# A four-layer decoder kernel: four batches in work in the first self-attention, and layer 1's cross weights prepared ahead

## The reference

```python
qkv = einsum('bsh,oh->bso', layernorm(x), w_qkv) + b_qkv
q, k, v = split(qkv, 3)
probs = softmax(q @ k.T / sqrt(256))
out = (probs @ v) @ w_out.T + b_out
```

## Time and profile before

| | us |
|---|---|
| median of 3 runs (lowest to highest) | 4235.8 (4234.36 to 4239.09) |
| profiled execution, its own time | 4226.08 |
| its span, first to last instruction | 4224.3 |
| mean granted clock of PE | 0.894 of full |
| `L0_attn` | 22.3 to about 200 |
| `L1_attn` | about 1124 to 1323 |
| `L1_xattn` before its first batch | 1323.6 to 1377.0 |

### The profile page before, as it was taken

One profiled execution on the slowest core, in us unless ns is written; L12 is line 12 of the kernel. 1 busy time (PEld: TensorE's weight loads), 2 busy tenths in 40 slices (PEclk: granted clock), 3 DMA queues, 4 the chain that ended last, 5 costly groups with the idle time before them and its releaser, 6 DMA issues. The chain is left out here.

```text
span 4224.3 us, 79122 instructions
## 1 busy us (share of the span) xinstructions
PE 3331.4 (79%) x29439; PEld 2439.1 (58%) x29440; DVE 2628.3 (62%) x6901; ACT 1752.5 (41%) x3882; POOL 102.1 (2%) x111
## 2 busy tenths in 40 slices
PE   5677777734485888988988989387997889768999
PEld 4545555411264556656656666166886767544788
DVE  4454454488667677777677766776884178577033
ACT  2234434357422566666666666133333244221011
POOL 0000000000001000000000000000110000000000
PEclk9899999855697999999999999698888999889599
DMA  2000000000300000000000000200000000023100
GB/s 88 13 16 20 21 16 21 7 0 0 127 11 10 2 1 2 1 1 2 1 2 1 1 2 1 86 0 11 15 15 1 0 1 0 27 73 90 42 9 11
DMA packets 85463, 79.13 MB, mean 19 GB/s; under 512 B 12496, under 2 KB 78640, under 8 KB 84784
## 3 DMA queue, kind: packets, MB, share of 16 engines
q1 hardware_dynamic: 84096, 75.57, 6.0%
q10 hardware_dynamic: 1200, 1.11, 0.1%
HBM read 74.57 MB, written 2.10 MB: 18 GB/s over the span
## 5 line engine op out<-in xcount | busy, mean ns | idle before, releaser
L2927 PE MATMUL bank<-L1w_w,L1x_xqT 128*128 128x512 f32 x640 | 303.2, 597 | 1.4 <-DVE L1x_xqT L3221 1.4
L2990 PE MATMUL bank<-L1w_wp,L1x_catT 128*128 128x256 f32 x1024 | 244.0, 381 | 12.0 <-ACT L1x_catT L3104 12.0
L1031 ACT ACTIVATE L0x_P<-bank,L0x_level 128x512 f32<-128x512 f32 x256 | 155.1, 688 | 189.9 <-PE bank L981 189.9
L3227 DVE TENSOR_REDUCE L1x_ssq<-L1x_square 128x4 f32<-128x512 f32 x192 | 131.6, 685 | 147.1 <-ACT L1x_square L3066 143.2
L3098 ACT ACTIVATE L1x_cat<-bank,L1x_osum 128x128 f32<-128x128 f32 x512 | 146.3, 369 | 170.1 <-DVE L1x_osum L3258 170.1
L2990 PEld LDWEIGHTS bank<-L1w_wp,L1x_catT 128*128 128x128 f32 x1024 | 186.8, 190 | 49.2 <-ACT L1x_catT L3104 15.0
L1047 DVE TENSOR_REDUCE L0x_top<-bank 128x4 f32<-128x512 f32 x256 | 158.9, 683 | 75.4 <-PE bank L959 73.7
L2975 PE MATMUL bank<-L1x_v,L1x_PT 128*128 128x129 f32 x1024 | 147.2, 286 | 65.4 <-ACT L1x_PT L3093 65.4
L3066 ACT ACTIVATE L1x_square<-bank 128x512 f32<-128x512 f32 x192 | 115.6, 602 | 160.9 <-PE bank L2927 160.9
L3076 ACT ACTIVATE L1x_hatT<-bank,L1x_affine 128x512 f32<-128x512 f32 x192 | 148.7, 774 | 71.1 <-PE bank L2949 69.0
L2949 PEld LDWEIGHTS bank<-ident,L1x_hat 128*128 128x128 f32 x768 | 91.0, 143 | 149.3 <-DVE L1x_hat L3237 114.0
(11 more groups left out here) (647 smaller groups left out, 8066.5 us busy)
## 6 DMA issues: line engine op xcount, KB each, us to landing
L0x_mask<-in_maskrows SPq DMA_DIRECT2D x16, 512.0 KB, 3.7
L3w_wg<-in_L_ffn_Wg SPq DMA_DIRECT2D x8, 704.0 KB, 8.5
L3w_wu<-in_L_ffn_Wu SPq DMA_DIRECT2D x8, 704.0 KB, 10.2
L1w_wp<-in_L_xattn_wproj SPq DMA_DIRECT2D x1, 4096.0 KB, 29.6
L3x_ctxT<-in_ctxT SPq DMA_DIRECT2D x32, 128.0 KB, 2.1
L3w_wd<-in_L_ffn_Wd SPq DMA_DIRECT2D x8, 512.0 KB, 10.0
...
```

The lines of the kernel that those rows point to most:

```text
L1031: act.activation(self.P[:, i % 2, r, :], self.work_bank[r][:, :], ACT.Exp, bias=self.level[:, :]).then_inc(self.p_ready.sem, 1)
L2927: last = pe.matmul(made_bank[n % 4][:, :], inputs(SOURCE[n], k), w[:, k, 4 * n:4 * n + 4, :], start=(k == 0), stop=(k == C - 1))
L2990: last = pe.matmul(y_bank[:, 0:D], catT[:, j, :], wp[:, 4 * m + j, :], start=(m == 0 and j == 0), stop=(m == MG - 1 and j == 3))
L3227: dve.tensor_reduce(ssq[:, 4 * n:4 * n + 4], square[:, n % 2, :].rearrange("p (h e) -> p h e", h=4), X, ALU.add).then_inc(sum_ready.sem, 1)
```

## The change

It does four things.

1. **`L0_attn`** is written in turns with a lead of three batches (`staged_by(eng, turn, 3)`: three turns in front, a loop of two turns run six times, four behind). In turn b PE turns xn(b+3), mixes b, scores b+1, projects b+2 in two halves with the transpose of o(b) between them, projects the output of b and transposes P(b+1). `norm_vector` moves from DVE to POOL. The bias of v moves behind the mix, where it is added in the instruction that scales o (`scalar_tensor_tensor`), and ACT instead of DVE copies v. The exponential is 2/(1-t) - 1.
2. In `masked_attention` (layers 1 and 2) and `L3_attn`, **`leaving.count` moves in front of `maxima_vector`**.
3. **The preparation of layer 1's cross part moves into `L1_attn`.** All small loads are issued there behind the big ones. In turns 1 to 12 DVE reduces the columns of eight heads of one half of w (the two turns of a pair take the same eight heads, one half each), and ACT subtracts the means from them, a head at a time. Turns 13 to 15 hold the reciprocals and small scales, turn 16 the rms of batches 0 to 14.
4. `smooth_rows` is spread by two DMAs through DRAM on the SyncE queue, in place of matmuls and copies. At the head of `L1_xattn` batch 0 starts at once, and the statistics of batch 15 are worked out between its steps.

```diff
 def L0_attn(kit):
+            def turn(b, odd, at_b):            # PE
+                here, scoring, entering, coming = 0 <= at_b, 0 <= at_b + 1 < B, 0 <= at_b + 2 < B, at_b + 3 < B
+                if coming:
+                    pe.wait_ge(normed.sem, normed.after(b + 3))
...
+                    turn_tensor(kit, pe, xT_out, kit.xn).then_inc(turned.sem, 1)
+                if here:
+                    pe.wait_ge(pT_ready.sem, pT_ready.after(b))
+                    pe.wait_ge(v_ready.sem, v_ready.after(b))
+                    pe.matmul(mix_out, PT[:, :], v[:, :], start=True, stop=True).then_inc(mixed.sem, 1)
...
+            pool.sem_inc(normed.sem, 1)
+            bias(0)
+            for b in range(1, B):
+                pool.wait_ge(turned.sem, turned.after(b - 1))
...
+                norm_vector(kit, pool, b, kit.xn[:, :]).then_inc(normed.sem, 1)
+                bias(b)
...
-                step(dve.scalar_tensor_tensor(P[:, :], P[:, :], 1.0, below[:, :], ALU.add, ALU.mult))
+                    step(dve.tensor_scalar(P[:, :], below[:, :], 2.0, -1.0, ALU.mult, ALU.add))
...
-                dve.tensor_scalar(o[:, :], bank[5][:, 0:D], inv[:, :], None, ALU.mult).then_inc(o_ready.sem, 1)
+                    dve.scalar_tensor_tensor(o[:, :], mix_out, inv[:, :], bv[:, :], ALU.mult, ALU.add).then_inc(o_ready.sem, 1)
...
 def masked_attention(kit, name, prefix, swap, meanwhile=None):
...
-                if ahead:
-                    at.maxima_vector(dve, b + 1, step)
                 if behind and at_b != B:
                     dve.wait_ge(y_read.sem, y_read.after(b - 1))
                     leaving.count(dve, b - 1)
+                if meanwhile is not None:
+                    meanwhile.prepare_vector(dve, step, b, at_b)
+                if ahead:
+                    at.maxima_vector(dve, b + 1, step)
...
 class L1xWeights:
+    CENTER_TURNS = range(1, 3)
+    def spread_smooth(self, sp):
...
+        sp.wait_ge(self.smooth_made, 1)
+        sp.dma_start(rows.rearrange("(h n) -> h n", n=self.D_HEAD), self.smooth_rows[:, :]).then_inc(self.smooth_kept, 16)
+        sp.wait_ge(self.smooth_kept, 16)
+        sp.dma_start(self.smooth[:, :, :].rearrange("p h n -> p (h n)"), row(rows).to_broadcast([128, 2 * self.NH * self.D_HEAD])).then_inc(self.smooth_spread, 16)
+    def prepare_vector(self, dve, step, b, at_b):
+        if at_b in self.CENTER_TURNS:
+            k, blocks = at_b - 1, bass.ds(b * 4 - 4 * at_b, 8)
+            dve.wait_ge(self.w_loaded, 16 * len(self.PARTS))
+            center = self.center[:, k, blocks]
+            step(dve.tensor_reduce(center, self.w[:, k, blocks, :], X, ALU.add))
+            dve.tensor_scalar(center, center, -1.0 / self.D_HEAD, None, ALU.mult).then_inc(self.centered, 1)
+        if at_b == B - 3:
+            dve.wait_ge(self.loaded, self.LOADS)
+            dve.reciprocal(self.smooth_rows[:, :], self.smooth_rows[:, :]).then_inc(self.smooth_made, 1)
...
+        for i in {B - 3: (0,), B - 2: (1, 2), B - 1: (3,)}.get(at_b, ()):
+            step(dve.reciprocal(self.in_inv[:, i, :], self.in_inv[:, i, :]))
+    def center_scalar(self, act, b, at_b):
+        if at_b in self.CENTER_TURNS:
...
+            for j in range(8):
+                head = bass.ds(b * 4 - 4 * at_b + j, 1)
+                act.activation(self.w[:, k, head, :], self.w[:, k, head, :], ACT.Identity, bias=self.center[:, k, head])
...
 def L1_xattn(kit):
             step.restart()
             scale_x(0, first=True)
             round_x(0)
+            dve.memset(v[:, :, d:d + 1], 1.0).then_inc(ones_made, 1)
+            pre_norm.vector(dve)
             turn_x(0)
             sum_squares(0, 0)
             enter(0)
+            pre_norm.finish(dve)
+            ahead.squares_vector(dve, step, B - 1, B, kit.meanvar, kit.rstd)
+            ahead.roots_vector(dve, step, B - 1, B, 2)
+            dve.wait_ge(ahead.smooth_spread, 16)
```

More of the change, by code:

```diff
@@ L557, in _ @@
+            staged_by(pe, turn, AHEAD)
         @block.scalar
         def _(act):
-            def turn(b):
-                act.wait_ge(turned.sem, turned.after(b))
-                act.copy(kit.xnT[:, :, :], bank[0][:, 0:D]).then_inc(xT_ready.sem, 1)
-            def batch(b, last=False):
-                if not last:
-                    turn(b + 1)
-                act.wait_ge(top_ready.sem, top_ready.after(b))
-                act.activation(P[:, :], bank[3][:, 0:128], ACT.Tanh, bias=top[:, :], scale=SCALE / 2).then_inc(tanh_ready.sem, 1)
-                act.wait_ge(p_turned.sem, p_turned.after(b))
-                act.copy(PT[:, :], bank[4][:, 0:128]).then_inc(pT_ready.sem, 1)
-                act.wait_ge(o_turned.sem, o_turned.after(b))
-                act.copy(oT[:, :, :], bank[6][:, 0:D]).then_inc(oT_ready.sem, 1)
@@ L1652, in L1_attn, with root_scalar, roots_vector @@
+    def root_scalar(self, act, lo, hi, turn):
+        act.wait_ge(self.squares, turn)
+        act.activation(self.rms[:, lo:hi], self.meansq[:, lo:hi], ACT.Sqrt, bias=self.eps[:, :]).then_inc(self.roots, 1)
+    def roots_vector(self, dve, step, lo, hi, turn):
+        dve.wait_ge(self.roots, turn)
+        step(dve.reciprocal(self.rms[:, lo:hi], self.rms[:, lo:hi]))
+        refine_vector(dve, step, self.rms[:, lo:hi], self.meansq[:, lo:hi], self.EPS, self.kit.newton[:, lo:hi])
 def L1_attn(kit):
@@ L3053, in _ @@
         def _(act):
-            pre_norm.scalar(act)
-            act.wait_ge(squares, 1)
-            act.activation(rms[:, :], meansq[:, :], ACT.Sqrt, bias=eps[:, :]).then_inc(roots, 1)
-            for m in range(MG):
-                act.wait_ge(smooth_spread, m + 1)
-                act.copy(smooth[:, 4 * m:4 * m + 4, :], flip_bank[m % 2][:, :]).then_inc(smooth_copied, 1)
-            act.wait_ge(prepared, 2)
+            act.wait_ge(ones_made, 1)
             def square_of(b, n):
```

317 lines of the change are left out of this document (154 added, 163 removed).

## The result

| | before | after |
|---|---|---|
| median, us (lowest to highest), 4 runs each | 4235.08 (4232.68 to 4239.09) | 4105.98 (4102.23 to 4106.98) |
| ratio, with its 95% interval | | 0.9693 (0.9676 to 0.9709) |
| the profiled execution's own time, us | 4226.08 | 4105.98 |
| its span, us | 4224.3 | 4104.2 |
| mean granted clock of PE | 0.894 | 0.902 |

The kernel is 129.1 us faster by the medians and 120.1 by the two profiled executions. The prediction said 4130, with a range of 4105 to 4165. The time is 24 us under the forecast and only 1 us inside the lower end of the range. The stages say where. A stage is counted here from its first instruction on DVE to that of the next one.

What follows compares the result with a forecast made beforehand. It took `L0_attn` as latency-bound, `L1_attn` as nearly PE-bound and the head of `L1_xattn` as serial. Terms -50-61-3+8 = -106 on 4226.1 gave 4120; adding 9.7 for the runs' median gave 4130 us, range 4105 to 4165.

Steps and rivals of the forecast that it cites:

- The bound of `L0_attn`, a relay: `L0_attn`: bound by latency, no engine full; DVE idles 1.77 us for the mix and 0.87 for y each turn.
- The term of `L0_attn`, -61: `L0_attn`: turns of 6.3 us, ending at 133.9 instead of 198.74, less 4 us for drops and warm-up; bounds -75 and -37.
- The norm on POOL: `L0_attn`: the norm moved from DVE to POOL takes 0.4 to 0.8 us, with a whole turn of lead.
- The head of `L1_xattn`, -50: Start of `L1_xattn`: 53.35 us go, 0.8 for statistics and 2 for finish and rms come back; bounds -47 and -52.
- Preparation in `L1_attn`, +8: `L1_attn`: 2.4 us for centering, less 0.5, plus 6.0 in the last turns; bounds +2 and +19.
- The term of ACT's centering: `L1_attn`, turns 1 to 12: ACT's eight activations delay the exponentials, costing 0.2 us a turn, 2.4 us in all.
- Statistics, -3 in `L2_attn`: `L2_attn`: statistics before the maxima bring oT earlier, 0.24 us a turn over 14 turns; bounds 0 and 5.
- (1) the half relay: `L0_attn`: DVE's one order makes waits add up to 8.0 us a turn, +24, 4154 us; chance 0.14.
- (2) ACT holds the mix: `L1_attn`: ACT's centering costs 0.9 us a turn instead of 0.2, +8 to 11, 4140 us; chance 0.10.
- (3) POOL blocks DVE: `L0_attn`: the port lock holds `below` and P for POOL's instructions, 1.4 us a turn, +20, 4150 us; chance 0.04.
- (4) POOL paces the stage: `L0_attn`: POOL's norm sets the turn; slower than before if a turn lasts 13.9 us; chance 0.02.
- (5) no effect: Loads or centering not ready, so `L1_xattn` waits as before, and `L0_attn` turns still go one by one; chance 0.02.

## Why the prediction was right, point by point

The mechanisms held, but the hit is narrow. Three terms were too cautious by 18 us together, the 9.7 us added to the sum had no ground in the kernel's code, and the range was wide enough below by 1 us. That it held is in part luck: the nine runs of the kernel after lie between 4102.2 and 4114.4 us, and the lowest is outside the range.

**The bound of `L0_attn`, a relay.** Right: with work of other batches ahead of each wait, DVE's 1.77 and 0.87 us went, and the clock rose, as the prediction argued from PE's busy share.

**The term of `L0_attn`, -61: mis-sized, it was -73.6 and -74.6 alone.** Four steps. The start: I charged 6 us at half clock for the third batch's projections, but its q and k ran at full clock (16 matmuls in 1.95 us, against 3.17 for the batch before), and turn 0 began at 33.9 instead of 36.5: -2.6. The turn: from the mix of turn 0 to that of turn 14, 79.7 us, 5.69 each instead of 6.3: -8.5. I had 0.8 us for the trip to ACT, which leaves DVE idle 0.44, and rounded 6.1 up to 6.3 for hand-overs that have no price when both sides find their work waiting. PE's own need was too high as well: I took the 6.18 of the earlier trace rows, and the same matmuls, with less waiting between them, are 5.41 of busy time. The prediction had named this overlap of modelled ends and given it only to the lower bound. The tail: 11.3 us instead of 9.2, since the last turns ran at half clock (y of batch 14 took 2.08 us, at full clock 1.03): +2.1. The allowance for drops in the loop: 4 us for none. -2.6-8.5+2.1-4 = -13, and -61-13 = -74. The half clock in the tail belongs to that execution: in its repeat and in the kernel with the new `L0_attn` alone the tail took 9.7 us. The lower bound of 5.6 us a turn was nearly the value: there was no reason to stand off from it once each wait had cover.

**The norm on POOL.** Its time was underestimated: 1.22 us where I bounded it by 0.4 to 0.8 from the two-input bias of 0.72. It did no harm, since a turn's lead is far longer. That it had to leave DVE was not argued in the prediction, and the runs show it is not so: in the gap of the tanh it costs 0.05 a turn.

**The head of `L1_xattn`, -50: right in the sum and in its parts.** The first step moved by the whole 53.35 us. From it to L3246 are 7.23 us, where there were 6.58 to L3221: +0.65 for the statistics, forecast 0.8. The stage as a whole is 50.64 shorter, which leaves 2.1 for the finish and the rms, forecast 2. This last agreement is no finer than some 3 us, since the stage took 1276.8 to 1280.1 in the kernels that have its code unchanged.

**Preparation in `L1_attn`, +8: measured +2.9.** The last turns were right: 12.58, 14.08 and 8.72 us against 10.65, 12.01 and 7.03 before are +1.9, +2.1 and +1.7, forecast +2.1, +1.9 and +1.7, and +0.3 up to the barrier, as forecast. The term of ACT's centering failed: 0.2 a turn, 2.4 in all, measured 0.0 with the activations left out. I took PE's need for P to be 0.4 us behind the old start; it was some 1.7 (0.33 by which the centering delays the exponentials and 1.3 beyond), because y lies between. DVE's 2.0 us in front of the maxima were 1.9, and did not make them late. And a turn of the kernel before, at 12.23 us where the kernel after has 10.51, had a stop of PE, at full clock, in the midst of its scores, that the kernel after did not have: 1.7 us of the gap are that. It comes before the next matmuls here:

```profile
1164.32 1.13 PE L1369 MATMUL bank<-L1a_kM,L1a_qT 32*128 32x256 f32 x11 [0.70 <-issue]
```

Its cause is open. The kernel with the old `L0_attn` and the new preparation has it too (0.65 us at the same place), so the preparation alone did not remove it. The eleven turns behind it gained 1.7 us together where the term had 0.5. With the 2.4 and the 1.7 above, this makes up the gap of 5.1. The +2.9 itself holds for one execution: with the same preparation the stage took 202.7 to 207.5 us, +2.2 to +7.0, by the clock in its last turns. Eight activations took 2.45 us; the 2.35 estimated from the Trainium skill, VectorE: DVE Perf Modes, section The TRN2 errata, were close.

**Statistics, -3 in `L2_attn`: measured -1.5, and -2.2 by the run that undid them.** The mechanism was right, the size of 0.24 a turn too large: of a pair of turns one became 0.17 shorter (10.68 to 10.51) and the other 0.01 (10.90 to 10.89). `L3_attn` 0, as forecast.

**Added to the sum.** I added 9.7 us, by which the runs' median stood above the profiled execution. The kernel after has both at 4105.98. The 9.7 belonged to that one execution of the kernel before and not to its code; by the profiles alone I would have said 4120, 14 too high, and the terms above account for those 14: -12.6-5.1-0.6+1.5+2.6, the last being the stages that nobody changed.

**The rivals.** (1) the half relay: out, 5.7 us a turn. (2) ACT holds the mix: out by the run without centering; it becomes true beyond 1.3 us more, and then costs more than the wait itself. (3) POOL blocks DVE: out in the loop, where `below` and P kept 0.23 us each, and for the reason that the prediction gave, that POOL is done before they start; the block itself exists (0.64 and 1.41 us in the rows above). (4) POOL paces the stage: out, it is busy 30.5 of 105.5 us. (5) no effect: out.
